# A second queue for part of the loads, one more slot for x, and the last stage's products spread evenly

## What is computed

```python
h = jax.nn.sigmoid(jnp.einsum('bts,st->bs', x, W1) + b1)
return h @ W2.T + b2
```

## Time and profile before

| | |
|---|---|
| median of 3 runs | 319.12 us (318.98 to 320.89) |
| the profiled execution | 320.03 us, of which the span 318.2 us |
| TensorE busy | 266.2 us (84%) |
| VectorE busy | 247.8 us (78%) |
| GpSimd busy | 215.1 us (68%) |
| ScalarE busy | 50.9 us (16%) |
| moved | 105.0 MB read, 4.2 MB written |
| granted TensorE clock, mean | 0.949 |

### The profile page before, as it was taken

How to read it: one execution, slowest core, us unless ns; L and a number is a source line. 1 busy time by engine, 2 the same in 40 slices (tenths; PEclk the granted TensorE clock), 3 DMA queues, 4 the chain that set the end, 5 groups by cost and what they waited for, 6 DMA issues and landing times.

```text
span 318.2 us, 4779 instructions
## 1 busy us (share of the span) xinstructions
PE 266.2 (84%) x1761; PEld 229.1 (72%) x1761; DVE 247.8 (78%) x368; ACT 50.9 (16%) x85; POOL 215.1 (68%) x125
## 2 busy tenths in 40 slices
PE   0957769478879999997799999589999959999594
PEld 0856659378758888887788887478888848888373
DVE  0729998549989888889869887967878985779925
ACT  4201214102270110010600000130111040000300
POOL 2219656555479999984999876499888589981000
PEclk9979999959999999999799999959999998999878
DMA  7999999999999999999999999999999999887007
GB/s 232 402 388 387 386 386 386 401 387 387 386 386 385 387 386 386 387 382 378 374 374 377 382 385 385 384 373 374 373 373 370 363 345 299 260 262 233 2 2 265
DMA packets 67675, 109.48 MB, mean 344 GB/s; under 512 B 3642, under 2 KB 40514, under 8 KB 67652
## 3 DMA queue, kind: packets, MB, share of 16 engines
q1 hardware_dynamic: 67056, 107.06, 94.5%
q10 hardware_dynamic: 596, 2.11, 1.6%
HBM read 104.97 MB, written 4.19 MB: 343 GB/s over the span
## 4 chain that ended last, share of the span: by engine, by line
PE 56%; DMA 29%; DVE 5%; issue 5%; ACT 2%; SPq 1%; DVEq 0%; ACTq 0%
DMA ring<-in_r_x 29%; PE xbank L227 27%; PE pbank L296 22%; DVE acc L346 3%; PE xbank L324 3%; PE pbank L324 1%; PE pbank L286 1%; DVE w_lo L353 1%; ACT h L421 1%; PE pbank L256 1%; ACT h_hi L446 1%; PE pbank L245 0%; DVE acc L344 0%; ACT L421 0%; SPq L190 0%
## 5 line engine op out<-in xcount | busy, mean ns | idle before, releaser
L346 DVE SCALAR_TENSOR_TENSOR acc<-xbank,w,acc 128x512 f32<-128x512 f32 x280 | 200.7, 746 | 45.1 <-PE xbank L227 37.3
L227 PE MATMUL xbank<-ident,ring 128*128 128x128 f32 x1184 | 175.8, 286 | 41.7 <-DMA ring<-in_r_x 35.2
L227 PEld LDWEIGHTS xbank<-ident,ring 128*128 128x128 f32 x1184 | 147.8, 148 | 71.2 <-issue 27.7
L475 POOL TENSOR_TENSOR nat<-nat,w1all 128x768 f32<-128x768 f32 (+2 forms) x56 | 107.0, 1912 | 60.6 <-DMA nat<-in_r_x 47.8
L485 POOL TENSOR_TENSOR nat<-nat 128x768 f32<-128x768 f32 (+2 forms) x46 | 87.7, 1906 | 3.6
L296 PE MATMUL pbank<-w_lo,h_hi 128*128 128x512 f32 x112 | 48.5, 433 | 0.0
L296 PE MATMUL pbank<-w_hi,h_hi 128*128 128x512 f32 x112 | 48.5, 433 | 0.0
L296 PE MATMUL pbank<-w_hi,h_lo 128*128 128x512 f32 x112 | 39.7, 427 | 0.0
L421 ACT ACTIVATE h<-acc,b1col 128x512 f32<-128x512 f32 (+1 forms) x22 | 12.5, 599 | 102.0 <-DVE acc L346 102.0
L340 DVE TENSOR_SCALAR acc<-xbank,w 128x512 f32<-128x512 f32 x16 | 12.0, 749 | 13.8 <-PE xbank L227 11.8
L296 PEld LDWEIGHTS pbank<-w_hi,h_hi 128*128 128x128 f32 x112 | 21.7, 194 | 0.9
(11 more groups left out here) (37 smaller groups left out, 98.8 us busy)
## 6 DMA issues: line engine op xcount, KB each, us to landing
ring<-in_r_x SPq DMA_DIRECT2D x38, 1024.0 KB, 13.3
ring<-in_r_x SPq DMA_DIRECT2D x36, 768.0 KB, 11.0
nat<-in_r_x SPq DMA_DIRECT2D x20, 512.0 KB, 13.1
nat<-in_r_x SPq DMA_DIRECT2D x24, 384.0 KB, 11.5
ring<-in_r_x SPq DMA_DIRECT2D x18, 512.0 KB, 5.2
y<-in_L_rec_W SPq DMA_DIRECT2D x2, 2048.0 KB, 15.0
nat<-in_r_x SPq DMA_DIRECT2D x12, 256.0 KB, 8.3
out_y<-y ACTq DMA_DIRECT2D x4, 512.0 KB, 6.5
```

What stands on the lines that cost most here:

```text
L227: mm = pe.transpose(xbank[u % XBANKS][:, j * P:(j + 1) * P], tile, ident[:, :])
L346: nc.vector.scalar_tensor_tensor(out=total, in0=bank, scalar=weight, in1=total, op0=ALU.mult, op1=ALU.add).then_inc(unit_added, 1)
L475: nc.gpsimd.tensor_tensor(slot, slot, row, ALU.mult).then_inc(nat_weighed, 1)
```

## The change

Four things. (1) `RING` goes from 5 to 6 slots and `NATS` from 6 to 4; a ring slot has twice the size of a `nat` slot. A part load then waits for sum m - 2. (2) The part loads leave SyncE's queue for ScalarE's, as `load_part`: the first four behind the first five row sets, 4 to 10 between copies of W2 and row sets, and in stages 1 to 4 from part 3 of the stage on, behind the stage's sigmoids, alternating with the copies L433 or the stores L437. The column `places` goes. (3) In the last stage the products of stage 3 are spread evenly over all 38 units but the first two, except for the last 12 matmuls (`REST`), which stand behind the last unit; VectorE's last two additions of these move behind the tail's splits. (4) The tail's outputs begin in the `xbank` banks and use `pbank` for the last two.

```diff
-    (0, 0, 4, 4, (2, 3, 5, 7, 9, 11, 13, 15, 17, 18), "keep"),
...
+    (0, 0, 4, 4, "keep"),
...
-    RING = 5
-    NATS = 6
+    RING = 6
+    NATS = 4
     XBANKS = 6
+    REST = 12
...
         def steps_due(i, v):
             steps = OUTS * steps_of(i - 1)
+            if i == LAST:
+                lead = chunks[i]
+                return max(0, -(-(v - lead + 1) * (steps - REST) // (len(units[i]) - lead)))
             lead = 2 * chunks[i]
-            span = len(units[i]) * (4 if i < LAST else 3) // 5 - lead
+            span = len(units[i]) * 4 // 5 - lead
...
-                    if at in places:
-                        s, k, f = parts[m]
...
-                        sp.dma_start(nat[:, m % NATS, :, :sn * P],
-                                     x_v[:, sj:sj + HALF, k, sc * P:(sc + sn) * P]).then_inc(nat_loaded[m % NATS], 16)
-                        m += 1
...
+            last_steps = OUTS * steps_of(LAST - 1)
+            for k in range(last_steps - REST, last_steps):
+                product_step(LAST - 1, k)
             for c in range(chunks[LAST]):
                 for n in range(OUTS):
                     j, cols = out_half(n)
-                    if c == 0 and n < 2:
-                        pe.wait_ge(y_added, added_at[LAST] - 1 + n)
-                    if c == 0 and n >= 2:
-                        pe.wait_ge(unit_added, UNITS - XBANKS + n - 2 + 1)
+                    if c == 0 and n < XBANKS:
+                        pe.wait_ge(unit_added, UNITS - XBANKS + n + 1)
+                    if c == 0 and n >= XBANKS:
+                        pe.wait_ge(y_added, added_at[LAST] - OUTS + n + 1)
...
+            for n in range(outs_due(LAST, len(units[LAST]) - 2), OUTS):
+                add_out(LAST - 1, n, pbank[n % 2])
...
+            def load_part(m):
+                s, k, f = parts[m]
+                if m >= NATS and parts[m - NATS][1] < pools[parts[m - NATS][0]] - 1:
+                    act.wait_ge(nat_added, sums_made(m - NATS + 2))
+                elif m >= NATS:
+                    act.wait_ge(unit_turned, sum_turned(parts[m - NATS][0]))
+                sj, sc, sn = STAGES[s][0] + HALF * f, STAGES[s][1], STAGES[s][2]
+                act.dma_start(nat[:, m % NATS, :, :sn * P],
+                              x_v[:, sj:sj + HALF, k, sc * P:(sc + sn) * P]).then_inc(nat_loaded[m % NATS], 16)
...
+            W2_PART = {3: 4, 7: 5, 11: 8, 15: 9}
+            SET_PART = {8: 6, 12: 7}
             for q in range(EARLY):
                 keep_set(q)
+            for m in range(4):
+                load_part(m)
             for m in range(SC):
                 high_w2(m)
+                if m in W2_PART:
+                    load_part(W2_PART[m])
             for q in range(EARLY, SETN):
                 keep_set(q)
+                if q in SET_PART:
+                    load_part(SET_PART[q])
             for m in range(SC, OH * SC):
                 high_w2(m)
+                if m in W2_PART:
+                    load_part(W2_PART[m])
+            load_part(10)
...
-                if i > 0 and fate[i - 1] == "keep":
-                    for n in range(OUTS):
...
+                if i > 0:
+                    first, end = first_part[i] + 3, min(first_part[i] + 2 * pools[i] + 3, len(parts))
+                    for m in range(first, end):
+                        load_part(m)
+                        at = m - first
+                        if i == 2 and at < JT:
+                            act.wait_ge(y_added, OH * (at + 1))
+                            act.dma_start(out_v[:, at, :], y[:, at, :]).then_inc(group_stored, 16)
+                        if fate[i - 1] == "keep" and at > 0 and at % 4 != 3:
+                            n = at - 1 - at // 4
+                            j, cols = out_half(n)
+                            if i > 1 and n == 0:
+                                act.wait_ge(group_stored, 16 * JT)
+                            act.wait_ge(out_summed, OUTS * (i - 1) + n + 1)
+                            nc.scalar.copy(y[:, j, cols], pbank[n % 2][:, :]).then_inc(part_kept, 1)
```

More of the change, by code:

```diff
@@ L19 @@
 STAGES = (
-    (0, 0, 4, 4, (2, 3, 5, 7, 9, 11, 13, 15, 17, 18), "keep"),
[L21 to L24, removed]
+    (0, 0, 4, 4, "keep"),
+    (0, 4, 4, 6, "last"),
+    (4, 0, 3, 6, "keep"),
+    (4, 3, 3, 6, "add"),
+    (4, 6, 2, 6, "last"),
 )
@@ L43, in rec_kernel @@
     pools = [s[3] for s in STAGES]
-    fate = [s[5] for s in STAGES]
+    fate = [s[4] for s in STAGES]
     NK0, NK = pools[0], max(pools)
@@ L179, in _ @@
                          W1.rearrange("(c p) t -> p c t", p=P)).then_inc(w1_loaded, 16)
-            m = 0
-            for i, (j0, c0, n, _, places, _) in enumerate(STAGES):
+            for i, (j0, c0, n, _, _) in enumerate(STAGES):
                 for at in range(T - pools[i]):
-                    if at in places:
-                        s, k, f = parts[m]
[L185 to L189, removed]
-                        sp.dma_start(nat[:, m % NATS, :, :sn * P],
-                                     x_v[:, sj:sj + HALF, k, sc * P:(sc + sn) * P]).then_inc(nat_loaded[m % NATS], 16)
-                        m += 1
                     q = item_of[i, pools[i] + at]
@@ L315, in _ @@
                     j, cols = out_half(n)
-                    if c == 0 and n < 2:
-                        pe.wait_ge(y_added, added_at[LAST] - 1 + n)
-                    if c == 0 and n >= 2:
-                        pe.wait_ge(unit_added, UNITS - XBANKS + n - 2 + 1)
+                    if c == 0 and n < XBANKS:
+                        pe.wait_ge(unit_added, UNITS - XBANKS + n + 1)
+                    if c == 0 and n >= XBANKS:
+                        pe.wait_ge(y_added, added_at[LAST] - OUTS + n + 1)
                     if n % OH == 0:
                         pe.wait_ge(tail_lo, c * JT + j + 1)
-                    bank = pbank[n] if n < 2 else xbank[(UNITS + n - 2) % XBANKS]
+                    bank = xbank[(UNITS + n) % XBANKS] if n < XBANKS else pbank[n - XBANKS]
                     for k, (a, w) in enumerate(((h_hi, w_hi), (h_hi, w_lo), (h_lo, w_hi))):
@@ L382, in _ @@
                                             ALU.subtract).then_inc(tail_lo, 1)
+            for n in range(outs_due(LAST, len(units[LAST]) - 2), OUTS):
+                add_out(LAST - 1, n, pbank[n % 2])
             for n in range(OUTS):
-                add_out(LAST, n, pbank[n] if n < 2 else xbank[(UNITS + n - 2) % XBANKS])
+                add_out(LAST, n, xbank[(UNITS + n) % XBANKS] if n < XBANKS else pbank[n - XBANKS])
         @block.scalar
@@ L468, in weigh @@
                 i, k, f = parts[m]
-                _, c0, n, _, _, _ = STAGES[i]
+                _, c0, n, _, _ = STAGES[i]
                 row = w1all[:, k, c0 * P:(c0 + n) * P].unsqueeze(1).to_broadcast([P, HALF, n * P])
```

## The result

The changed kernel takes 371.24 us (median of 4 runs, 369.73 to 371.75) against 319.22 us before: 1.162 times, 95% interval 1.158 to 1.166. 343 us was predicted, 327 to 362 as the range. The direction and the place were right, the size was not: 24 us were forecast and 52 came.

The account below looks back on a forecast made before the run. The prediction took transfers as the bound until some 260 us, then TensorE. With late sums, the last read at 317.5 us, sigmoid at 325.6 and 16.1 of tail, the span was 341.7; plus 1.8, less 0.9: 343 us, range 327 to 362.

Parts of the forecast that it names:

- The wait that decides: Stage 2, ScalarE's queue: part 7 stands behind four output stores, the last waiting for stage 1's products until 208.1 us.
- Stage 0 and 1: First two stages: the first loses nothing; in the second, late parts delay TensorE's reading of the sums by 11.5 us.
- L: Time from issue to landing of a part load: 6.5 us in stage 1, 3.5 to 4 from stage 2 on.
- Stage 2: After the stores: landing 3.5 us, five parts 18.6 us; TensorE reads the sum at 230.2 us, 31.3 late.
- Stage 3: From the previous stage's sum to this one's: 48.9 us, with landing 4 and eight parts at 3.85 us.
- Stage 4: Last stage, from the previous sum to its own: 38.4 us, with landing 3 and eight parts at 2.8 us.
- (L + work)/2: Part loads with four slots: two in flight, so a part takes this time or GpSimd's own work, whichever is larger.
- slow landings: Rival: parts land in 6.5, 5.5 and 4.5 us by size throughout; time 366 us; chance 0.2.
- The round-robin rule: Part loads: transfer engines alternate between queues, so a 512 KB part takes some 4.1 us; the trace didn't bear this out.
- the quick rival: Rival: part landings near the idle row, 2.4 and 2.1 us; stage 1 not late; time 328 us; chance 0.25.
- The end: After the last sum: 8.1 us to the sigmoid, which waits for the 12 matmuls, then a 16.1 us tail.
- The last stage's gain: Last stage: even spreading without late sums ends TensorE at 290 to 291 us, worth 8 us, but hidden by GpSimd.

Follow-up runs that it names:

- stores_behind: The changed kernel with the four output stores of stage 2 moved behind all part loads of that stage on ScalarE; 350.6 us.
- quarter_x: The changed kernel, but each x item loads only its first 128 rows, a quarter of the bytes, which TensorE transposes four times; 316.8 us, one run.
- last_only: The kernel before with only the last stage changed: even products, 12 matmuls behind the last unit, banks of the tail; 315.2 us, ratio 0.988.
- last_only_r0: The kernel before with the last stage's products spread evenly and no matmuls kept behind the last unit (`REST` 0); 313.7 us.

## Why the prediction was wrong
**The wait that decides: right.** Stores and parts alternate, part 7 was issued at 210.46 us (208.1 forecast), and stores_behind gives its price, 20.6 us.

**Stage 0 and 1: right in time.** Between 106 and 155 us a 512 KB part landed in 6.4 us, for 6.5. The period of a part was 5.53 us (weighs from 108.30 to 152.56) for 5.65; n(1) at 158.5 for 155.2, because the low parts ended 3.2 us later, behind parts 1 and 2. That no transfer would be lost yet was wrong: from 143 to 158 us they ran at 220 GB/s.

**The step that failed is L "from stage 2 on, where a late sum leaves all six x slots full and the transfer engines partly idle".** I took 3.5, 4 and 3 us for stages 2, 3 and 4. The rows show:

- Stage 2: part 7 landed after 7.5 us, not 3.5: 4 us.
- Stage 3: part 3 was issued at 246.6 behind the last rounded copy and weighed at 254.87, 8.3 us later, not 4. The period was (291.99 - 254.87)/8 = 4.64, not 3.85. Together 4.3 + 6.3 = 10.6 us: the stretch from n(2) to n(3) was 59.5 us for 48.9.
- Stage 4: period (340.21 - 311.22)/8 = 3.62 for 2.8, part 3 6.0 us behind the copy for 3: 47.1 us for 38.4.

These 4, 10.6 and 8.7 us, with 3.3 from stage 1 and 2.4 from the end, make 29; 1 us was regained in stage 2, and the span came 27.9 us above the 341.7 forecast. The reasoning mixed up two moments. The stretch in which part 7 was under way, and one behind it (columns as in the earlier trace rows: the last three are the clock, the transfer engines' share and GB/s):

```profile
210.46:218.00 7.54, 0.00 (x0) 0.00 (x0) 0.89 (x2) 0.00 (x0) 0.26 (x2) 0.78 0.97 340
222.00:230.00 8.00, 0.00 (x0) 0.00 (x0) 0.00 (x0) 0.00 (x0) 7.84 (x5) 0.50 0.38 98
```

TensorE already stands, but x issued before and a store are still under way: share 0.97. The engines go idle (0.38) only once part 7 has landed. There the short landing of the forecast did come:

```profile
nat<-in_r_x ACTq DMA_DIRECT2D x4, 384.0 KB, 3.2
```

These are the four part loads issued from 221 to 236 us. But GpSimd had work for 3.64 us per part, so their landing was hidden and gained nothing. The next part that counts is issued after the late sum, when the six slots come free one after the other and x is loaded at the full rate. The stretch in which stage 3's first late part was under way:

```profile
246.60:254.90 8.30, 8.30 (x56) 7.07 (x55) 8.23 (x13) 1.21 (x2) 3.45 (x4) 1.00 1.06 379
```

Share 1.06 at 379 GB/s: no idle engine. Full engines aren't the whole of a long landing, though: the part issued at 272.83 us took 6.9 us to its weigh at a mean share of 0.75, and in the first 3.1 us, at 0.64, not one packet of ScalarE's queue moved. In the idle stretch the first packet came 1.0 us after the issue. What sets this start is open.

quarter_x put the short landings in by force and got the stretches that the forecast had (47.4 and 37.0 for 48.9 and 38.4), so the terms around L were right: with its landings of 3.4 and 2.9 us the same sums give 47.3 and 37.9. The formula (L + work)/2 holds roughly: with the median landings of 6.0 and 4.6 us it gives 4.85 and 3.6, for 4.64 and 3.62 measured. The rival "slow landings" had 56.4 and 45.9 for them and 366 us; even it was low, by the 8.3 us landings at a stage's start. Its chance of 0.2 was the error of judgement: "late sums empty the transfer engines" was no reason against it.

**The round-robin rule.** By the rule of the Trainium skill (DMA: Bandwidth & Descriptors, "Queues, rings and completion order"), that each transfer engine takes turns between the queues, the prediction estimated 4.1 us for a 512 KB part; it put this with the quick rival, whose own terms are 2.4 and 2.1. The trace has 7.3 beside a full x queue and 4.2 in quarter_x, where a quarter of x is loaded: the estimate fits engines with room, not full ones.

**The end: nearly right.** n(4) to the sigmoid took 10.3 us for 8.1, because TensorE had stood for 14.25 us and began at the lower clock (granted 0.50 from 343 to 347 us); the tail then ran at the full clock, 16.4 us for 16.1. That the sigmoid waits for the 12 matmuls is shown by last_only and r0.

**The last stage's gain: oversized.** 8 us were forecast for it alone, 3.5 measured. The step left the transfers out: it set TensorE's end at 290 to 291 us without asking whether the last bytes, which come at 288 us, leave it time for the rest. With nothing kept behind the last unit, last_only_r0 gained 5.4.

## What to carry to other kernels
A load in the queue of a computing engine inherits every wait ahead of it, so look for the last event that the queue must see before the load, and count the work that still stands behind the load. When slots are taken away, the time per piece is about (landing + work)/2 with two in flight, and the landing to put in is that at the moment of issue: here the transfers were full both when the stall began and when it had ended, and idle only between. Where spreading work evenly removes one bound, check at once the next by its bytes.

## What was not expected of the hardware
A 512 KB part took 7.3 us to land beside x with six x slots and with three (a 384 KB one 6.0 and 5.2), but 4.2 us when x was a quarter as many bytes: the landing went with the bytes that run, much less with the number of loads queued. And a second queue neither cost nor gave bandwidth: 313.5 us with parts in ScalarE's queue, 313.7 with all in SyncE's.
